# Finishing a norm inside the combine loop, and moving half of another norm's work to GpSimd

## What is computed

```
def _layernorm(x, axis=-1, eps=1e-05):
    m = jnp.mean(x, axis=axis, keepdims=True)
    v = jnp.var(x, axis=axis, keepdims=True)
    return (x - m) / jnp.sqrt(v + eps)

    # layer 0's mixture, then layer 1's first block
    x = x + _L0_ffn_ref(_layernorm(x, axis=-1), ...)
    h = rmsnorm(_layernorm(x), g_res)                 # inside _L1_xattn_ref
    h = jnp.einsum('bld,ed->ble', h, W_in) + b_in

    # inside _L2_ffn_ref, x being _layernorm(x) of the running sum
    h = _rms(x, n1_w)
    heads = lambda w_: (h @ w_.T).reshape(B, T, HEADS, HD).transpose(0, 2, 1, 3)
    q = _rms(heads(wq), qn_w)
    k = _rms(heads(wk), kn_w)
    v = heads(wv)
    ...
    x = x + ao
```

## Time and profile before

| | us |
|---|---|
| median of 3 runs (lowest, highest) | 3170.71 (3170.32, 3171.92) |
| the profiled execution, its own time | 3168.09 |
| its span, first to last instruction | 3166.2 |
| PE busy in the span | 2538.6 (80%) |
| DVE busy | 2188.5 (69%) |
| ACT busy | 1274.6 (40%) |
| POOL busy | 990.4 (31%) |

### The profile page before, as it was taken

One profiled execution on the slowest core, in us unless ns is written; L12 is line 12 of the kernel. 1 busy time (PEld: TensorE's weight loads), 2 busy tenths in 40 slices (PEclk: granted clock), 3 DMA queues, 4 the chain that ended last, 5 costly groups with the idle time before them and its releaser, 6 DMA issues. The chain is left out here.

```text
span 3166.2 us, 57355 instructions
## 1 busy us (share of the span) xinstructions
PE 2538.6 (80%) x21348; PEld 1656.4 (52%) x21348; DVE 2188.5 (69%) x5562; ACT 1274.6 (40%) x2273; POOL 990.4 (31%) x1412
## 2 busy tenths in 40 slices
PE   1998385999904497997989876886699999969982
PEld 1443263666604266886556543444466555656662
DVE  5997763666557764675678767997766545867757
ACT  1777353333202323111346654773222222256622
POOL 3442271110074260113656326871300000024330
PEclk9999598999956698998999997998799999979996
DMA  3331266221150147665721022100100000011001
GB/s 96 131 110 69 96 232 204 80 79 62 41 158 12 65 168 259 226 229 183 233 79 48 12 74 81 43 23 5 64 10 13 1 1 1 1 39 48 29 10 58
DMA packets 158167, 266.90 MB, mean 84 GB/s; under 512 B 22635, under 2 KB 106137, under 8 KB 151876
## 3 DMA queue, kind: packets, MB, share of 16 engines
q1 hardware_dynamic: 131204, 186.97, 17.8%
q0 software_dynamic: 17904, 76.23, 7.1%
q10 hardware_dynamic: 8784, 0.04, 0.2%
HBM read 175.25 MB, written 88.34 MB: 83 GB/s over the span
## 5 line engine op out<-in xcount | busy, mean ns | idle before, releaser
L1495 ACT ACTIVATE l2e_hf<-l2e_H 128x512 f32<-128x512 f32 x208 | 124.2, 597 | 381.4 <-PE l2e_H L1451 381.4
L1626 POOL TENSOR_TENSOR all_m_rstd<-all_m_sq,all_mhalf 128x8 f32<-128x8 f32 x24 | 39.6, 1648 | 557.4 <-DVE all_m_sq L1611 523.0
L772 DVE TENSOR_REDUCE l0a_mx<-l0a_S 128x2 f16<-128x512 f32 x256 | 168.0, 686 | 21.7 <-PE l0a_S L606 21.0
L1533 DVE CAST l2e_hh<-l2e_hf 128x512 f16<-128x512 f32 x208 | 92.7, 446 | 122.9 <-ACT l2e_hf L1495 108.6
L721 ACT ACTIVATE l0a_pf<-l0a_ST 128x512 f32<-128x512 f32 x256 | 146.6, 602 | 53.1 <-PE l0a_ST L620 52.9
L768 DVE CUSTOM_DVE_ANT_0 l2s_masked<-l2s_S,l2s_mq 128x128 f32<-128x128 f32 (+1 forms) x512 | 153.3, 349 | 20.4 <-PE l2s_S L606 19.9
L1451 PE MATMUL l2e_H<-l2o_hi,l2e_w 128*128 128x512 f16 x576 | 151.4, 381 | 15.8 <-DVE l2e_w L1509 15.8
L1495 ACT ACTIVATE l0e_hf<-l0e_H 128x512 f32<-128x512 f32 x128 | 76.4, 597 | 206.1 <-PE l0e_H L1451 206.1
L1451 PE MATMUL l2e_H<-l2e_hh,l2e_w 128*128 128x512 f16 x640 | 155.1, 379 | 0.0
L1535 DVE TENSOR_TENSOR l2e_hl<-l2e_hf,l2e_hh 128x512 f16<-128x512 f32 x208 | 147.3, 708 | 7.2
L1451 PE MATMUL l1e_H<-l1b_hi,l1e_w 128*128 128x256 f16 (+1 forms) x936 | 144.8, 274 | 7.8 <-DMA l1e_w<-packed,all_second_weight_row 7.8
(11 more groups left out here) (711 smaller groups left out, 7508.3 us busy)
## 6 DMA issues: line engine op xcount, KB each, us to landing
l0e_wf<-in_L_ffn_w SPq DMA_DIRECT2D x16, 1024.0 KB, 7.7
rows<-l0a_zeros SPq DMA_DIRECT2D x16, 640.0 KB, 5.9
l1u_rb<-rows SPq DMA_DIRECT2D x20, 512.0 KB, 5.0
results<-l1e_y SPq DMA_DIRECT2D x39, 256.0 KB, 3.4
l0a_kv<-in_ctx SPq DMA_DIRECT2D x16, 512.0 KB, 4.1
rows<-l0a_zeros SPq DMA_DIRECT2D x16, 512.0 KB, 4.9
l0d_p_cx<-in_ctx SPq DMA_DIRECT2D x16, 512.0 KB, 6.4
l0u_rb<-rows SPq DMA_DIRECT2D x16, 512.0 KB, 5.1
```

The source lines that it names most:

```text
L772: m = nc.vector.tensor_reduce(mx[h % 2][:, :, i], ps[:, :].rearrange("p (u k) -> p u k", u=TB), AX.X, ALU.max)
L1495: nc.scalar.activation(hf[q % 4][0:fn, :], pair_of(q, lay)[0][0:fn, :], lay.func, scale=1.0 / WS).then_inc(acted, 1)
L1533: nc.vector.tensor_copy(high, v).then_inc(hi_done, 1)
L1626: self.nc.gpsimd.tensor_tensor(out=(self.rstd, self.rstd2)[which][:, g], in0=(self.sq, self.sq2)[which][:, g], in1=self.g.mhalf[:, 0:self. ...
```

## The change

Three things:

1. In l1n (`by_act`) the statistics of tile t-1 are made between the two adds of tile t, and each quarter is rooted, seconded and applied as soon as its last tile is added. The lo parts of a quarter are written in the middle of the next one's adds. ScalarE takes, quarter by quarter, both roots, the odd tiles and the hi parts.
2. l2m makes only the doubly normed output (`kind="ln_rms2"`), and in halves: even tiles on VectorE, odd ones on ScalarE. GpSimd scales the weights by the gains there (`gained`). `xin` is written by GpSimd in l2q, four tiles ahead of each group's query multiplications.
3. l2q has groups of QT = 4 tiles instead of 8, no scaling ahead of `wh`, PE waits for `wh` only, and the products with `wl` come last in each accumulation, so that only the first one waits for `wl`.

```diff
@@ class Norm @@
+    def tile(self, dve, t):
+        self.nc.vector.bn_stats(self.stats[:, t, :], self.src[:, t, :]).then_inc(self.stats_done, 1)
+    def gather(self, dve, t):
+        dve.wait_ge(self.stats_done, t + 1)
+        self.nc.vector.bn_aggr(self.mv[:, t, :], self.stats[:, t, :]).then_inc(self.mv_done, 1)
+        if t % self.GQ == self.GQ - 1:
...
+            self.nc.vector.tensor_scalar(self.sq[:, g], self.mv[:, g, 1], LN_EPS, None, ALU.add
+                                         ).then_inc(self.root_in[0], 1)
@@ on_vector @@
+        if self.by_act:
+            for q in range(self.NQ):
+                before(dve, q)
+                self.invert(dve, 0, q)
+                self.second(dve, q)
+                self.invert(dve, 1, q)
+                self.apply(dve, q)
+            self.lo_parts(dve, self.NQ - 1)
+            return
@@ on_pool @@
             self.root(pool, 1, 3)
+            if self.finish is not None:
+                self.finish(pool, self.fetched)
             return
@@ on_scalar @@
+        if self.by_act:
+            for q in range(self.NQ):
+                self.act_root(act, 0, q)
+                self.act_root(act, 1, q)
+                self.odd_tiles(act, q)
+                for n in range(q * self.GQ // TB, (q + 1) * self.GQ // TB):
+                    self.hi_part(act, n)
+            return
...
-            if self.rms_out is not None and (n + 1) % (self.GQ // TB) == 0:
-                q = n // (self.GQ // TB)
-                act.wait_ge(self.off_set, q + 1)
-                for t in range(q * self.GQ, (q + 1) * self.GQ):
-                    self.nc.scalar.activation(self.out[:, t, :], self.src[:, t, :], ACT.Identity,
-                                              bias=self.off[:, t:t + 1], scale=self.rstd[:, t:t + 1])
@@ def qkv_stage @@
-    HEADS, dh, QT, QN, AHEAD = 16, D // 16, 8, NT // 8, 3
+    HEADS, dh, QT, QN, AHEAD = 16, D // 16, 4, NT // 4, 3
-                    if t % QT == 4 and t >= QT:
+                    if t % QT == 2 and t >= QT:
                         keep_keys(t // QT - 1)
-                pe.wait_ge(w_lo, 1)
+                pe.wait_ge(w_hi, 1)
-                        for x, w in ((hi, wh), (hi, wl), (lo, wh)):
+                        for x, w in ((hi, wh), (lo, wh), (hi, wl)):
+                            if t == 0 and w is wl and done is a_done:
+                                pe.wait_ge(w_lo, 1)
-                act.wait_ge(w_scaled, KD)
             @block.gpsimd
             def _(pool):
+                _, mean, _, _, rstd, _ = g.moments
                 for n in range(QN):
+                    for t in range(n * QT, (n + 1) * QT):
+                        nc.gpsimd.tensor_scalar(xin[:, t, :], g.x[:, t, :], mean[:, t, 0:1], rstd[:, t:t + 1],
+                                                ALU.subtract, ALU.mult)
                     pool.wait_ge(rt_set, n + 1)
             @block.vector
             def _(dve):
-                for k in range(KD):
-                    nc.vector.tensor_scalar(wf[:, k, :], wf[:, k, :], gains[:, k:k + 1], None, ALU.mult
-                                            ).then_inc(w_scaled, 1)
-                dve.wait_ge(w_scaled, KD)
@@ def combine_stage, add @@
+                        if norm.by_act and t % norm.GQ:
+                            if n % 2 == 0:
+                                dve.wait_ge(added, n)
+                                norm.tile(dve, t - 1)
+                            else:
+                                norm.gather(dve, t - 1)
+                        if norm.by_act and q and n % 16 == 9:
+                            norm.lo_parts(dve, q - 1)
                     dve.wait_ge(added, (q + 1) * 2 * norm.GQ)
+                    if norm.by_act:
+                        norm.tile(dve, t)
+                        norm.gather(dve, t)
@@ def self_layer @@
+                def gained(pool, fetched):
+                    pool.wait_ge(fetched, 16 * len(fetch))
+                    for k in range(KD):
+                        nc.gpsimd.tensor_scalar(wf[:, k, :], wf[:, k, :], gains[:, k:k + 1], None, ALU.mult)
```

More of the change, by code:

```diff
@@ L127, in place @@
         self.fetched = st.sem("n_fetched")
-        if self.rms_out is not None or self.halved:
+        if self.halved:
             self.off, self.off_set = st.sb("n_off", [P, NT]), st.sem("n_off_set")
@@ L228, in apply @@
             m.then_inc(self.normed, 1)
-        if self.rms_out is not None:
-            nc.vector.scalar_tensor_tensor(self.off[:, g], self.mv[:, g, 0], -1.0, self.rstd[:, g],
-                                           ALU.mult, ALU.mult).then_inc(self.off_set, 1)
     def lo_parts(self, dve, q):
```

51 lines of the change are left out of this document (22 added, 29 removed).

## The result

The changed kernel takes 3135.95 us (median of 4 runs, 3133.99 to 3139.26); the kernel before takes 3170.52 beside it (4 runs, 3167.71 to 3171.92). The ratio is 0.9893, with a 95% interval of 0.9876 to 0.9910: 34.6 us faster, where 34.5 was forecast (3136 us). The interval allows 28.5 to 39.3 us, so it is luck that the two agree to 0.1; what tests the prediction are the lengths of the stages.

A forecast was written before the change was run, and what follows sets the result against it. Bounds were l1n's norm behind the last add, ScalarE's xin tiles in l2m, and PE with its waits in l2q. Savings 18.3 + 5.1 + 2.9 + 6.3 + 2.3 = 34.9, taken as 34.5 from 3170.71: 3136 us, range 3131 to 3148.

The forecast's parts named there:

- Part 1, l1n: l1n: last add stays at 959.2 to 959.7, norm behind it shortens, next stage at 970.5; 18.3 us saved.
- rival B: l1n: VectorE sets the gathers' pace, statistics between adds costing 0.2 more each, 5 us in all; 3141 us, chance 0.10.
- Part 2, l2m: l2m: from 27.0 us to l0gn's 21.1 plus 0.8, so 21.9; 5.1 us saved, range 3 to 5.5.
- Part 3, the head: Start of l2q: scaling and wait for wl gone, PE starts 1.6 us in, first matmuls cover wl; 2.9 us saved.
- Part 4, groups of four: l2q: norms of four tiles no longer stop PE; of 7.8 us lost, 6.3 saved, 1.5 left for VectorE's lag.
- Part 5, the tail: l2q behind PE's end: small operations, keys' multiplication, query multiplications and keys' store shrink; 2.3 us saved, range 0 to 4.
- 1.3 for that delay: l2q's tail: group 6's norm, two tiles ahead of PE's end, delays the last sums by some 1.3 us.
- a little for `xin` still on GpSimd: l2q's tail: small unitemised allowance, with which the saving of 2.6 by the keys was taken as 2.3 us.
- 0.7 for `xin`: l2q: GpSimd's assumed price in us per xin, nearest the same shape; a group then takes 6.1 of 7.8, covered.
- Rival A: l2q: GpSimd and VectorE hold each other up, one us per norm, some 6 in all; 3142, up to 3148; chance 0.17.
- Rival C: l2q: GpSimd's price per xin lengthens the stage; no gain at 2.4 us, 3188 at 3 us; chance 0.03.
- Rival D: l1n: change does less than said, late gathers or ScalarE's order delaying a root; 2 us at most, inside the range.

The follow-up runs named there:

- head_old: Changed kernel with l2q's head as before: VectorE scales the weights there, PE waits for wl, wl products second; 3219.71 us against 3248.16 for the kernel before.
- l2m_full: Changed kernel with l2m not halved: VectorE makes all 32 tiles of its output, ScalarE only the hi parts; 3217.61 us.
- qt8: Changed kernel with l2q's groups of eight tiles again (QT = 8); 3225.85 us against 3248.16 for the kernel before.
- xin_ahead: Changed kernel with GpSimd writing xin two groups ahead, so none stands before the last query multiplications; 3219.51 us, ratio 0.9901 to the kernel before.
- xin_twice: Changed kernel with GpSimd writing each group's four xin a second time; 3249.25 us against 3248.16 for the kernel before.

## Why the prediction was right

**Part 1, l1n.** Every step is in the rows: last add at 959.76 (forecast 959.2 to 959.7), apply at 964.69 (964.3), PE at 965.51 (965.2), next stage at 970.82 (970.5). The account of VectorE, 20 of 20.2 us in a quarter, held on this chip with waits of 0.3. That it leaves no margin was rival B's point; its price of up to 5 us is about what the other chips take back, in traces that show stops there.

**Part 2, l2m.** 22.0 us against 21.9 forecast, from l0gn's 21.1 and 0.8. The weights' scaling was priced at 0.9 to 2.2 each and took 2.2, the upper end; it held up VectorE in one quarter, as foreseen, and in `head_old` no cost of this is seen. The prediction put the difference to l0gn down to ScalarE's 32 tiles of `xin`; `l2m_full` bears it out for all but about 1 us.

**Part 3, the head.** PE starts 1.54 into the stage (1.6), 3.1 us saved for 2.9. The matmuls that were to cover `wl` did not quite: it came 0.9 us too late for the third pair and cost the first tile some 0.5 (4.03 instead of 3.58).

**Part 4, groups of four.** 65.4 us of PE, forecast 64 to 66, and no wait of PE for the queries over 0.2. `qt8` shows the mechanism: with eight the three stops are back, 5.4 us of wait. Priced at 8.1 of VectorE's time for each group against PE's 7.8, the two were called level; the window has 18.89 of 20 beside PE's 20.00, or 7.4 for each 7.8. So there was more room than the prediction counted on.

**Part 5, the tail**, is the mis-sized term: 1.6 saved instead of 2.3. By the keys' store, the path that the prediction summed, its terms read as follows. The keys' multiplication saved 1.06 (forecast 1.1) and the store 1.45 (1.4; from its issue 4.04 now and 5.49 before). The small operations saved 1.0 instead of 1.4 (3.23 now, 4.26 before). The last sums were delayed by 2.0 instead of 1.3 (3.33 behind PE's end, 1.34 before): group 6's norm ran from 1874.48 to 1878.16, 3.7 where 3.4 had been priced, and two tiles' sums had to follow it. **So the step that failed first is the 1.3 for that delay**, by 0.7. The second is "a little for `xin` still on GpSimd": 0.4 on the small operations, which `xin_ahead` gives back while the 3.3 us delay stays. It comes with the price of **0.7 for `xin`**, which is 1.24 in the median and 1.29 in the mean, so that four take 5.51 in the tail and the last queries start 2.3 us after they could. They end 0.94 before the next stage starts, as in `xin_twice` (0.95), where they alone end the stage: so in the changed kernel they have caught up with the store, but put the end off by less than 0.1 (store to next stage 4.04, against 3.97 in `xin_ahead`). The row taken for the price was that of the same shape with two tensors (0.725); none of the three rows was of the same form. The upper end of the price, 1.65, held. By the prediction's own formula 1.24 gives an l2q of 18.5 + 7 x (3.3 + 4.96) + 4.9 = 81.2, under the 89.8 before (it measured 78.8), so the error in the price did not endanger the forecast; but GpSimd's group is then 7.9 (4.95 and 2.95) against PE's 7.8, where 6.1 had been expected. What was called covered had no slack left. That it just fitted was luck.

**Rival A** happened in the small. GpSimd's query multiplications are 2.95 a pair beside the keys' multiplication of 1.23, instead of 2.07. VectorE's small operations on 128 columns take 0.40 to 0.56 instead of 0.23 to 0.29 where they start in the first 0.3 us of an `xin`; those that start later in it are not slowed. The one most often hit, in six of the eight norms, is L2126 (duration in ns: least, median, most):

```profile
L2126 DVE TENSOR_SCALAR l2q_z<-l2q_z x8: 227/466/467, 1829.2 to 1882.4; 128x128 f32<-128x128 f32 x8
```

Each of the slowed ones ends 0.69 behind the start of the `xin` (L2124 at 1881.63 for 0.40, L2127 at 1882.67 for 0.56, `xin` at 1881.34 and 1882.55), as if the 1.24 us instruction held VectorE up in its first 0.4 only. Beside GpSimd's query multiplications it is otherwise: in `xin_twice` such an operation (L2133 there is L2127 of the changed kernel) takes up to 1.06 and ends 0.15 behind a query multiplication of 1.06:

```profile
L2133 DVE TENSOR_TENSOR l2q_rt<-l2q_rt,l2q_z x8: 291/293/1059, 1906.4 to 1963.4; 128x128 f32<-128x128 f32 x8
```

The Trainium skill (SBUF — State Buffer, section Who interferes with whom) has the two take one shared port in turn, whoever is first for its whole instruction. The traces now agree that each waits for the other, and for the whole length beside a query multiplication; beside `xin` VectorE's wait is shorter than that. (`L2126` has one tensor input only; it is slowed all the same.) So a norm loses some 0.2 us in the middle of the stage and 0.4 in the tail, far from the 1 us that the rival needed. (The rival's own sum is a little high: eight times 1 less 3 is 5, not 6.)

**Rival C** is 1.2 us per `xin` away: `xin_twice` stands near where the rival put the point of no gain. **Rival D** (ScalarE's order) did not show on the first chip: the root at 961.16 waited for VectorE.

## What to carry to other kernels

Work that a loop makes ready piece by piece should be finished in the loop, as long as the engine that finishes it has time left there: of four quarters of a norm three went under the gathers and 18.6 of 29.6 us behind them were gone. A periodic chore that stops the bounding engine is better done twice as often at half the size, so that each stop fits into the lead that the buffers give: 5 to 7 us of PE's time from one constant. And when work is moved onto an idle engine, add up that engine's group against the bounding one's with the price of the very form of instruction: here 1.24 against an assumed 0.7 just fitted, and with every `xin` written twice the whole gain of the change was lost.
